# A two-layer mixture of experts with attention, a gated scan and two MX-FP6 linears: four sets of tail buffers, another rounding, and transfers asked for in another order

## The reference

```python
x = x + 0.5 * ffn(layernorm(x))            # 8 experts, top 2, 128 -> 512 -> 128, relu
x = x + attn(layernorm(x))                 # 16 heads of 8, rotary, causal
x = x + 0.5 * ffn(layernorm(x))            # the same experts again
x = x + 0.5 * mx(layernorm(x))
x = x + gated(x)
x = x + 0.5 * mx(layernorm(x))

def mx(x):   # per 32 features: scale = max|x| / 7.5, round x / scale to the FP6 E2M3 grid
    return (nearest_on_grid(x / scale) * scale) @ wq.T + bias     # wq: weight, rounded alike

def gated(x):
    xn = rmsnorm(x, rms_mix_w)
    g, v, d = xn @ Wg.T + bg, xn @ Wv.T + bv, xn @ Wd.T + bd
    a = 0.001 + 0.998 * sigmoid(d)
    h = scan(h = a * h + sigmoid(g) * tanh(v))     # along the positions
    x = x + h
    xn = rmsnorm(x, rms_ffn_w)
    return x + (silu(xn @ W_gate.T) * (xn @ W_up.T)) @ W_out.T    # 384 wide
```

## Time and profile before

| | us |
|---|---|
| median of 3 runs | 1385.29 |
| lowest and highest | 1380.07, 1401.86 |
| profiled execution | 1396.99 |
| its span | 1395.3 |
| PE busy | 1012.7 |
| DVE busy | 873.2 |
| ACT busy | 628.3 |
| POOL busy | 537.5 |

### The profile page before, as it was taken

One profiled execution on the slowest core, in us unless ns is written; L12 is line 12 of the kernel. 1 busy time (PEld: TensorE's weight loads), 2 busy tenths in 40 slices (PEclk: granted clock), 3 DMA queues, 4 the chain that ended last, 5 costly groups with the idle time before them and its releaser, 6 DMA issues.

```text
span 1395.3 us, 21086 instructions
## 1 busy us (share of the span) xinstructions
PE 1012.7 (73%) x6869; PEld 717.2 (51%) x6869; DVE 873.2 (63%) x2457; ACT 628.3 (45%) x1341; POOL 537.5 (39%) x730
## 2 busy tenths in 40 slices
PE   1058885879899997799899648989991386664273
PEld 1048875655655764346567635646571356643132
DVE  5536474647665767457564446866659777858646
ACT  2135653345464664345467324636751363452241
POOL 2424245227221125565122472332428722344312
PEclk9999997899898998589899869968995698886576
DMA  9958987664554533534355756714114243410000
GB/s 334 353 211 289 320 297 238 210 222 145 164 173 137 171 108 87 175 113 133 107 167 192 262 153 192 239 61 135 54 54 158 68 152 117 163 29 14 15 0 16
DMA packets 84461, 217.33 MB, mean 156 GB/s; under 512 B 14848, under 2 KB 43392, under 8 KB 69760
## 3 DMA queue, kind: packets, MB, share of 16 engines
q1 hardware_dynamic: 76160, 199.18, 42.6%
q0 software_dynamic: 8192, 16.79, 4.1%
HBM read 160.86 MB, written 54.53 MB: 154 GB/s over the span
## 4 chain that ended last, share of the span: by engine, by line
PE 52%; DVE 11%; DMA 11%; issue 9%; POOL 8%; ACT 5%; SPq 4%; POOLq 0%; DVEq 0%; ACTq 0%
PE bank L584 46%; PE bank L596 5%; POOL z_scratch L1481 4%; DMA Qs<-q_scratch 4%; DMA q_scratch<-ab 2%; DMA tb<-in_wr 1%; DMA zin<-z_scratch 1%; SPq L542 1%; POOL yg L1493 1%; DVE sm_m L1090 1%; SPq L554 1%; DMA z_scratch<-zb,pos 1%; ACT tb L1277 1%; DMA k_scratch<-ab 1%; PE bank L731 1%
## 5 line engine op out<-in xcount | busy, mean ns | idle before, releaser
L1090 DVE TENSOR_REDUCE sm_m<-bank 128x4 f32<-128x512 f32 x320 | 212.1, 684 | 114.2 <-PE bank L584 113.9
L1515 POOL TENSOR_SCALAR_AFFINE_SELECT P<-P 128x256 f32<-128x256 f32 (+1 forms) x320 | 118.7, 377 | 348.4 <-ACT P L1367 344.8
L1367 ACT ACTIVATE P<-bank 128x512 f32<-128x512 f32 x320 | 179.8, 598 | 104.2 <-PE bank L584 103.4
L584 PE MATMUL bank<-zh,wt 128*128 128x256 f32 x1272 | 203.5, 310 | 14.9 <-DVE zh L1021 5.8
L1029 DVE SCALAR_TENSOR_TENSOR hlo<-bank,hhi 128x512 fp32r<-128x512 f32 x212 | 144.4, 687 | 101.9 <-ACT hhi L1316 101.2
L584 PEld LDWEIGHTS bank<-zh,wt 128*128 128x128 f32 x1272 | 178.8, 210 | 27.5 <-issue 12.3
L1316 ACT ACTIVATE hhi<-bank 128x512 fp32r<-128x512 f32 x212 | 125.9, 598 | 102.8 <-PE bank L584 97.2
L584 PE MATMUL bank<-hhi,wt 128*128 128x256 f32 x848 | 160.1, 313 | 5.4 <-ACT yb L1324 5.4
L1481 POOL DMA_INDIRECT z_scratch<-zb,pos x128 | 128.8, 1006 | 84.3 <-DVE pos L1010 49.2
L1493 POOL DMA_INDIRECT yg<-y_scratch,pos x128 | 124.6, 974 | 90.6 <-issue 54.1
L584 PE MATMUL bank<-Ks,Qs 32*128 32x256 f32 (+2 forms) x512 | 110.3, 447 | 66.7 <-DMA Qs<-q_scratch 53.6
(11 more groups left out here) (184 smaller groups left out, 1694.6 us busy)
## 6 DMA issues: line engine op xcount, KB each, us to landing
wt<-w_scratch SPq DMA_DIRECT2D x106, 1025.0 KB, 6.5
zin<-z_scratch SPq DMA_DIRECT2D x106, 128.0 KB
y_scratch<-yt SPq DMA_DIRECT2D x106, 128.0 KB
w_scratch<-wt SPq DMA_DIRECT2D x8, 1024.0 KB, 9.3
q_scratch<-ab SPq DMA_DIRECT2D x32, 256.0 KB
k_scratch<-ab SPq DMA_DIRECT2D x32, 256.0 KB
Ks<-k_scratch SPq DMA_DIRECT2D x64, 128.0 KB, 2.8
Qs<-q_scratch SPq DMA_DIRECT2D x64, 128.0 KB, 3.1
```

The lines of the kernel that those rows point to most:

```text
L584: return e.matmul(o, lhs, rhs, start=start, stop=stop, **kw)
L1090: e.tensor_reduce(bn_m[:, k, s_, :], blocks(shared("maxi", i, 0, s_)), AX.X, ALU.max).then_inc(*d_max.step(i, f"m{s_}"))
L1367: e.activation(P[:, (2 * i + s_) % PR, :], shared("scor", i, 0, s_), ACT.Exp, scale=SCALE).then_inc(*a_sc.step(i, f"e{s_}"))
L1515: e.affine_select(out=v, in_=v, compare_op=ALU.is_ge, fill=0.0, base=0, channel_multiplier=-1, pattern=pattern).then_inc(*p_sc.step(i, f"m ...
```

## The change

It has five parts.

- Head. The raw weights of seven experts have a place of their own (four in P as before, three in xs 2 to 7, whose inputs come later; the last rows in tb, ob, hd and ab), so that all loads are asked for at once (the eighth waits for the first split). The zero fills of the first phase's part of z_scratch follow behind them, the rest behind zin of block 5. The inputs of batches 2 to 7 and the weights of attention and tail (`later()`) are asked for behind the last write of split weights. The ones in Ks are set by DVE in proj(0) and no longer at the start. route compares with six multiples of a block's size and not with four.
- Tails. TAIL_LANE gives the eight batches four sets of buffers, of five tiles each; sets 2 and 3 lie in P and can be used once the last *val* of the attention is done.
- nearest. A step size is taken from the exponent bits of u (bitwise_and with 0x7F800000, at least 1), and two roundings with a magic constant, one of u and one of u plus a small offset, are joined by a minimum: seven steps, on signed values, so ACT's abs goes.
- The bias of mx is no longer added by POOL but by PE, with a matmul of 128x512 (a matrix `top` with one row of ones, times biasb) ahead of those with wdT. In gated, the sum of squares of z2 comes from four ACT Squares with accumulation, and DVE's stats of it go.
- The table. All lengths in STAGES are others, the default lateness is 0.12 and not 0.15, and mxb of an earlier batch has a head start (LAST). With these nearly every row of the order of every engine has another place.

```diff
+def pieces_of(f, start, end):
+    return [(f, i, min(1024, end - i)) for i in range(start, end, 1024)]
+FIRST_FILL = pieces_of(0, 0, PHASE[0].blocks * SB)
+LATER_FILL = pieces_of(0, PHASE[0].blocks * SB, SLOTS) + pieces_of(1, 0, SLOTS)
+EB = -(-TILES * 128 // SB)
+TAIL_LANE = (0, 1, 0, 2, 3, 1, 0, 2)
+TAILS = max(TAIL_LANE) + 1
+def lane_before(b):
+    return max([p for p in range(b) if TAIL_LANE[p] == TAIL_LANE[b]], default=-1)
 WROW = 2048 + 2
 WR = 4
 PR = 10
-SG = 4
+SG = 7
...
-    "scat": ("G2.2+3", [], 1),
-    "wload": ("S.3+6", [], 1),
...
+    "scat": ("G2.55+2.5", [], 1),
+    "wload": ("S2.6+4", [], 1),
+    "stack": ("S1.8+3.5", [], 1),
...
+LAST = 15.0
...
-        return [("split", u - SG, 2)]
+        return []
     if stage == "split":
         return [("sload", u, 0)] if k == 0 else [("split", u - WR, 3)] if k == 1 else []
     if stage == "prep":
         if k == 0:
-            return [("prep", u - 2, 9)] + ([("heads", USES[u][1], 3)] if USES[u][0] == 2 else [])
+            return [("prep", u - 2, 9)] + ([("heads", USES[u][1], 3)] if USES[u][0] == 2 else [("split", NE - 1, 3)] if u > 1 else [])
...
+        if k == 3 and TAIL_LANE[u] >= 2:
+            return [("val", NB * NG - 1, 2)]
+        return [("comb", 4 * UNIT[2, u] + 3, 1), ("mxb", lane_before(u), 12)] if k == 0 else [("wquant", 0, 4)] if k == 11 else []
...
+            rest = LAST * (NB - 1 - x[1]) if x[0] == "mxb" else 0.0
+            left[x] = share + late + max([left[y] for y in after.get(x, ())], default=rest)
...
-        tb = [[sb(f"tb{i}{j}", [128, 4, 128]) for j in range(6)] for i in range(2)]
+        tb = [[sb(f"tb{i}{j}", [128, 4, 128]) for j in range(5)] for i in range(2)]
+        lane_t = [[t[:, :, :] for t in lane] for lane in tb]
+        lane_t += [[P[:, 5 * i + j, :].rearrange("p (j c) -> p j c", c=128) for j in range(5)] for i in range(2)]
...
+            return (flat(tb[1][2]), flat(tb[1][3]), flat(tb[1][4]), flat(tb[0][4]), ob[:, :], flat(hd), ab[0][:, :])[n % SG]
+        def raw_weights(n):
+            i = n % SG
+            return P[:, 2 * i:2 * i + 2, :] if i < 4 else xs[:, 2 * i - 6:2 * i - 4, :, :].rearrange("p a j d -> p a (j d)")
...
-                w.wait_ge(*p_init.at(0, "zero"))
-                for f in range(2):
-                    for i in range(0, SLOTS, 1024):
-                        n = min(1024, SLOTS - i)
-                        e.dma_start(zd[f][i:i + n].rearrange("(p j) d -> p j d", p=128), zeros[:, 0:n // 128, :]).then_inc(l_zero, 16)
                 w.wait_ge(l_first, 64)
                 e.dma_start(wd[:, 2048:WROW].rearrange("(e p) c -> p e c", p=128), bt).then_inc(s_bias, 16)
+            def fill(parts, done):
+                w.wait_ge(*p_init.at(0, "zero"))
+                for f, i, n in parts:
+                    e.dma_start(zd[f][i:i + n].rearrange("(p j) d -> p j d", p=128), zeros[:, 0:n // 128, :]).then_inc(done, 16)
...
-                e.dma_start(P[:, 2 * (n % SG):2 * (n % SG) + 2, :], a["w12"][n]).then_inc(l_raw[n % SG], 16)
+                e.dma_start(raw_weights(n), a["w12"][n]).then_inc(l_raw[n % SG], 16)
                 e.dma_start(last_row(n), a["wr"][n]).then_inc(l_raw[n % SG], 16)
-                if n == 3:
-                    later()
+                if n == NE - 1:
+                    fill(FIRST_FILL, l_zero0)
                 yield
             def split(n):
                 w.wait_ge(*d_split.at(n, "lo"))
                 e.dma_start(wd[128 * n:128 * n + 128, 0:2048], wt[n % WR][:, 0:2048].bitcast(F32)).then_inc(s_w[n % WR], 16)
+                if n == NE - 1:
+                    later()
...
+                if u == 5:
+                    fill(LATER_FILL, l_zero)
...
+                    mm(blocks(o), top[:, :], biasb.unsqueeze(1).to_broadcast([128, 4, 128]), True, False, skip_group_check=True)
                     w.wait_ge(*a_wq.at(0, "w"))
                     w.wait_ge(*a_mx[v].at(b, "zt"))
                     for j in range(4):
-                        t = mm(o[:, j * 128:(j + 1) * 128], t_[1][:, j, :], wdT[:, :], j == 0, j == 3, skip_group_check=True)
+                        t = mm(o[:, j * 128:(j + 1) * 128], t_[1][:, j, :], wdT[:, :], False, j == 3, skip_group_check=True)
...
-            def nearest(f, u_, bufs):
-                u, p, q, st, r = bufs
-                e.tensor_scalar(p, r, 2.0, 0.125, ALU.is_ge, ALU.mult).then_inc(*f.step(u_, "p"))
-                e.tensor_scalar(q, r, 4.0, 0.25, ALU.is_ge, ALU.mult).then_inc(*f.step(u_, "q"))
-                w.wait_ge(*f.at(u_, "q"))
-                e.scalar_tensor_tensor(out=st, in0=p, scalar=0.125, in1=q, op0=ALU.add, op1=ALU.add).then_inc(*f.step(u_, "st"))
-                w.wait_ge(*f.at(u_, "st"))
-                e.scalar_tensor_tensor(out=p, in0=st, scalar=MAGIC, in1=u, op0=ALU.mult, op1=ALU.add).then_inc(*f.step(u_, "r1"))
-                w.wait_ge(*f.at(u_, "r1"))
-                e.scalar_tensor_tensor(out=r, in0=st, scalar=-MAGIC, in1=p, op0=ALU.mult, op1=ALU.add).then_inc(*f.step(u_, "r2"))
-                yield
+            def nearest(f, u_, u, r, t):
+                e.tensor_scalar(r.bitcast(U32), u.bitcast(U32), 0x7F800000, None, ALU.bitwise_and).then_inc(*f.step(u_, "p"))
+                w.wait_ge(*f.at(u_, "p"))
+                e.tensor_scalar(r, r, 1.0, None, ALU.max).then_inc(*f.step(u_, "e"))
+                w.wait_ge(*f.at(u_, "e"))
+                e.scalar_tensor_tensor(out=t, in0=r, scalar=MAGIC / 8, in1=u, op0=ALU.mult, op1=ALU.add).then_inc(*f.step(u_, "r1"))
+                yield
+                e.scalar_tensor_tensor(out=u, in0=r, scalar=(MAGIC + 1) / 8, in1=u, op0=ALU.mult, op1=ALU.add
+                                       ).then_inc(*f.step(u_, "r2"))
                 w.wait_ge(*f.at(u_, "r2"))
-                e.tensor_tensor(p, r, u, ALU.subtract).then_inc(*f.step(u_, "d1"))
-                w.wait_ge(*f.at(u_, "d1"))
-                e.scalar_tensor_tensor(out=q, in0=p, scalar=2.0, in1=st, op0=ALU.mult, op1=ALU.is_ge).then_inc(*f.step(u_, "d2"))
-                w.wait_ge(*f.at(u_, "d2"))
-                e.tensor_tensor(q, q, st, ALU.mult).then_inc(*f.step(u_, "d3"))
-                w.wait_ge(*f.at(u_, "d3"))
-                e.tensor_tensor(r, r, q, ALU.subtract).then_inc(*f.step(u_, "d4"))
+                e.scalar_tensor_tensor(out=u, in0=r, scalar=-0.125, in1=u, op0=ALU.mult, op1=ALU.add).then_inc(*f.step(u_, "r3"))
+                w.wait_ge(*f.at(u_, "r3"))
+                e.scalar_tensor_tensor(out=t, in0=t, scalar=1.0, in1=u, op0=ALU.mult, op1=ALU.min).then_inc(*f.step(u_, "mn"))
+                w.wait_ge(*f.at(u_, "mn"))
+                e.scalar_tensor_tensor(out=t, in0=r, scalar=-MAGIC / 8, in1=t, op0=ALU.mult, op1=ALU.add).then_inc(*f.step(u_, "r"))
...
-                w.wait_ge(*f.at(b, "z2"))
-                stats(T[0], sm_, f, b, ("bn3", "ag3"))
-                w.wait_ge(*f.at(b, "ag3"))
-                e.tensor_tensor(t_, mv[:, :, 0], mv[:, :, 0], ALU.mult).then_inc(*f.step(b, "t4"))
-                w.wait_ge(*f.at(b, "t4"))
-                e.tensor_tensor(t_, t_, mv[:, :, 1], ALU.add).then_inc(*f.step(b, "t5"))
-                w.wait_ge(*f.at(b, "t5"))
-                e.tensor_scalar(t_, t_, 1e-6, None, ALU.add).then_inc(*f.step(b, "t6"))
+                yield
+                w.wait_ge(*a_ga.at(b, "sq"))
+                e.tensor_scalar(t_, t_, 1.0 / D, 1e-6, ALU.mult, ALU.add).then_inc(*f.step(b, "t6"))
...
+                w.wait_ge(*d_ga.at(b, "z2"))
+                for j in range(4):
+                    t = e.activation(T[4][:, j, :], T[0][:, j, :], ACT.Square, accum_out=sm_[:, 44 + j:45 + j])
+                t.then_inc(*f.step(b, "sq"))
...
-                    e.tensor_tensor(x, x, hbias.unsqueeze(1).to_broadcast([128, 4, 128]), ALU.add).then_inc(*f.step(b, "x"))
```

More of the change, by code:

```diff
@@ L191, in timetable @@
             for k, step in enumerate(steps):
-                queues.setdefault((stage, u % lanes, step[0]), []).append((u, k))
+                lane = TAIL_LANE[u] if stage in ("mxa", "gated", "mxb") else u % lanes
+                queues.setdefault((stage, lane, step[0]), []).append((u, k))
     before, after = {}, {}
@@ L1261, in gated @@
                 w.wait_ge(*p_ga.at(b, "x"))
[L1262 removed]
+                e.tensor_tensor(x, x, blocks(shared("gated", b, 38)), ALU.add).then_inc(*f.step(b, "x"))
                 yield
```

215 lines of the change are left out of this document (113 added, 102 removed), and 40 rows, old and new, of the table STAGES.

## The result

| | before | after |
|---|---|---|
| median, us | 1389.09 (4 runs) | 1290.67 (4 runs) |
| lowest and highest | 1380.07, 1401.86 | 1272.37, 1295.09 |
| profiled execution, its span | 1396.99, 1395.3 | 1272.37, 1270.6 |
| last write of a block's y on ACT | 1235.4 | 1097.5 |

The ratio is 0.9253, with an interval from 0.913 to 0.9377: faster, by some 7.5%. (In the medians the difference is 98 us. The two profiled executions lie 125 us apart, because the one of before is slower than its median and the one of after is the fastest of its kernel.

The account below looks back on a forecast made before the run. No engine full: DMA-bound head, PE-bound middle, bubble, then an end of serial chains. Last block 1229.5 - 10 - 20 - 45 - 38 = 1116.5, plus 170 gives 1286.5, with 1.7 outside 1288; beside the median 1276 us, range 1232 to 1336.

Parts of the forecast that it names:

- Head, -10: Start, bound by DMA: zero fills and fourth block's weights go behind the first zin; -10 us (-2 to -14).
- Middle, -20: 210 to 1045 us: POOL's step for k and q stands behind fewer scatters, shortening the 25.4 us wait; -20 us (0 to -25).
- New waits for Qs or zin in the middle: Sign of being wrong: PE newly waiting for Qs or zin in the middle; no size given.
- Bubble, -45: 1045 to 1110 us: last route gets seven blocks as cover, so PE's idle time goes; -45 us (-15 to -50).
- 38 of tail work moved behind: Last block ends earlier as mx and gated work on PE moves behind it: 43 us, of which 38 counted.
- Lighter rounding and sums: nearest with seven steps for nine, -37 us of DVE; z2's statistics moved to ACT, -13 us of DVE.
- The first rival: Behind the last block, DVE and POOL steps hold each other up: 28 us more, 1304 us; chance 0.18.
- The end, 170 us behind the last block: Behind the last block DVE is the bound, with 153 us of work at 90% busy: 170 us (160 to 195).
- a busy share under 80%: Sign of being wrong: DVE under 80% busy at the end would mean the chains are still serial.
- I take 90% including the last chain alone: Behind the last block: DVE's assumed busy share with up to four chains in flight, turning 153 us of work into 170.
- The rival that the lanes bring nothing: Tail: written order still puts pairs after one another, so only the savings and the head stay: 1338 us; chance 0.10.
- The slower one: Attention: loads of q and k become PE's wait, +137 us on the forecast, 1413 us; chance 0.05.

Follow-up runs that it names:

- old_head: Changed kernel with the old start (all zero fills first, four raw buffers), order built anew: 0.9318 of before, where the changed kernel has 0.9256.
- table_only: Kernel before with the new lengths, default lateness and head start of early mxb alone; old instructions, head and two buffer sets: 0.971 of before, by the medians.
- table_lanes: Changed kernel with both the table's old lengths (old lateness, no mxb head start) and two sets of tail buffers: 0.9699 of before.
- two_lanes: Changed kernel with two sets of tail buffers in place of four: 0.9445 of before.
- old_table: Changed kernel with the table's old lengths and default lateness and no head start for early mxb: 0.9581 of before.
- no_bias: Changed kernel without the bias product on PE (output lacks the bias), same order: 0.9307 of before.

## Why the prediction was right, and where it wasn't

1276 us were forecast, beside a median of 1385.3; measured is 1290.67, within the range, and -98 us by the medians where -109 were summed. (The sum itself was made on profiled executions and gave 1288; that of the changed kernel took 1272.37, so stretches read from its trace come out shorter than its median would have them, by some 18 us in all.)

*Head, -10.* Right: the first zin came 12 us earlier, block 15 came 9.8 earlier. That it is all kept to the end isn't shown (old_head: some 9 us, within the interval's width).

*Middle, -20.* The mechanism was right and the size too small. The waits for Qs fell from 53.6 to 5.0 us, the hole of 25.4 is gone, and at block 91 the kernel is 46 us ahead where head and middle had 30. That the place in the order makes this wait is shown by table_only (1.7 us with the new order and the old instructions) and by table_lanes (31.1 us in its whole trace, one wait of 13.2). New waits for Qs or zin in the middle were named as a sign of being wrong: five for zin, 9.2 us, stand from 210 to 930 us, a small price beside the 49 us gained.

*Bubble, -45, and 38 of tail work moved behind.* Together 83 between block 91 and the last block; measured 92. Only the two together can be read from the trace. two_lanes shows that this stretch needs the sets: with two, it is 48 us longer and the one behind it 36 shorter. The order alone isn't enough: with the new lengths and two sets table_only still takes 182 us there, and with the old lengths and four sets old_table takes 98.

*Lighter rounding and sums.* DVE's busy time fell by 47, where -37 and -13 were summed. The steps of nearest, 1000 us to the end, in the lanes that lie in tb (line, form, count, busy, mean ns, idle before), and the new product of PE:

```profile
...
L638 PE MATMUL bank<-small,top 128*128 128x512 f32 x28 | 17.0, 694 | 0.0
...
L1218 DVE SCALAR_TENSOR_TENSOR tb<-tb 128x512 f32<-128x512 f32 x8 | 6.5, 810 | 0.3
...
L1214 DVE SCALAR_TENSOR_TENSOR tb<-tb 128x512 f32<-128x512 f32 x8 | 5.6, 696 | 0.3
...
L1209 DVE SCALAR_TENSOR_TENSOR tb<-tb 128x512 f32<-128x512 f32 x8 | 5.5, 693 | 0.3
L1216 DVE SCALAR_TENSOR_TENSOR tb<-tb 128x512 f32<-128x512 f32 x8 | 5.5, 692 | 0.3
...
L1211 DVE SCALAR_TENSOR_TENSOR tb<-tb 128x512 f32<-128x512 f32 x8 | 5.5, 685 | 0.0
...
L1205 DVE TENSOR_SCALAR tb<-tb 128x512 uint32<-128x512 uint32 x8 | 4.1, 508 | 0.4 <-POOL tb L1582 0.4
...
L1207 DVE TENSOR_SCALAR tb<-tb 128x512 f32<-128x512 f32 x8 | 3.4, 427 | 0.3
...
```

The seven means make 4.51 us against 4.34 forecast and 6.64 before; in P they make 4.41. PE's product has two records of 0.69, and 17.0 / 14 = 1.2 us of busy time, more than the 0.8 taken, and nothing in the result (no_bias).

*The first rival, DVE and POOL holding each other up, 28 us.* It falls for the steps of nearest: 0.1 to 0.2 us for each nearest are what it costs, 2 to 3 us in all. The new order has less of such meetings than the old, where they cost about 0.95 us in each. The row on L1158 had shown that the meeting is dear; how often it happens hangs mostly on the order. Take what the means of a nearest's steps add up to beyond its undisturbed steps (5.68 us for the nine, 4.30 for the seven). table_only, which keeps POOL's bias step and has the new order, pays 0.24 us for each nearest; old_table, which lacks the bias step and has the old order, pays some 0.6.

*The end, 170 us behind the last block.* 173 were measured, by luck: two errors cancel. DVE had 132 us of work there and not 153: though PE's steps of eleven mx and six gated are still to come when the last block ends, DVE starts only ten of the roundings and five of the scans behind it. And it was busy 76% and not 90%: 90% until 1170, as forecast, and 67% in the last 100 us. There fewer batches are left than there are sets, and the chain of each sets the time; in the whole end DVE waits 21.6 us, in eight waits, for products of PE. I had named a busy share under 80% as the sign that the chains are still serial. That sign came true over the whole end. The step that failed is "I take 90% including the last chain alone". It leaned on a slice of the kernel before where DVE was busy 77% (1268 to 1320 us); over that kernel's whole end it was 105 of 160 us, 66%. So the new kernel brought it from 66 to 76%. A smaller slip: PE's last product of the last block ended at 1233.0 before, and not "some 6 earlier" than 1235.8.

*Which way it went.* The rival that the lanes bring nothing (1338) falls by two_lanes, though the two more sets are worth 0.012 to 0.019, and so less than the order. The slower one, waits for q and k, falls by their 5.0 us. The last block came at 1097.5, earlier than the 1115 to 1130 named. A part of the whole isn't assigned: at 0.97 (both undone) 0.030 are left for head, rounding and sums, whose single runs give 0.006 each and at most 0.006 for the sums. Whether the rest, some 0.012, is POOL's removed bias, the sum being more than its parts as DVE comes closer to the bound, or the spread of the runs, stays open. It wasn't tried to put the bias back on POOL. Nor is the part of the clock separated: behind the last block TensorE's granted clock was 0.64 before and 0.83 after, and PE's products with wga on the tb sets took 759 and 650 ns in the mean there (730 on the sets in P). PE was idle for more of that stretch before (88 of 160 us against 59 of 173), so this may be a consequence of the fuller order; how much of the gain it carries no run shows.

## What to carry to other kernels

In a program whose engines each follow a fixed order, the table that builds it can be worth as much as the code: here it was worth about 0.03 with the old instructions and with the new, as much as all that is left at 0.97. A wait behind one late step shows as idle time of the bounding engine, with the releaser an engine that isn't busy (here POOL, at 39%). When a wait is gone or comes back, look at where it stands: the same row held expert blocks with two sets and only the end with four. And price a saving by the stretches in which it stands: of 28 us taken off DVE in the old order only those behind the last block showed, some 9, while 22 us added in the new order cost 22.
